# A Mamba layer with a mixture of experts on one core: gather and scatter moved in GpSimd's row, y's gating moved to the third stage, down weights in runs of 4 KB, x loaded a step ahead

## What is computed

```python
xn = layernorm(x)
# Mamba
u, gate = split(xn @ in_proj_w.T)
u = silu(conv4(u) + conv_b)                      # per channel, over the tokens
ts, B, C = split(u @ x_proj_w.T)
dt = softplus(ts @ dt_proj_w.T + dt_proj_b)
state[t] = state[t-1] * exp(dt * A) + dt * B * u # 16 states for each of 1024 channels
y = sum_over_states(state * C) + u * D
mamba = (y * silu(gate)) @ out_proj_w.T
# experts: for each (token, expert) pair among the top 6
moe = sum(score * (silu(xe @ w_gate) * (xe @ w_up)) @ w_down)
shared = (silu(xn @ sw_gate) * (xn @ sw_up)) @ sw_down
out = x + mamba + moe + shared
```

## Time and profile before

| | |
|---|---|
| median of 3 timed runs | 1342.65 us (1342.62 to 1343.42) |
| profiled execution | 1335.79 us, its span 1334.0 us |
| mean granted TensorE clock | 0.988 |
| busy: TensorE, VectorE, ScalarE, GpSimd | 1254.7, 1079.7, 899.2, 866.5 us |
| moved by DMA | 305.64 MB, mean 229 GB/s |

### The profile page before, as it was taken

How to read it: one execution, slowest core, us unless ns; L and a number is a source line. 1 busy time by engine, 2 the same in 40 slices (tenths; PEclk the granted TensorE clock), 3 DMA queues, 4 the chain that set the end, 5 groups by cost and what they waited for, 6 DMA issues and landing times.

```text
span 1334.0 us, 52998 instructions
## 1 busy us (share of the span) xinstructions
PE 1254.7 (94%) x21558; PEld 804.3 (60%) x21558; DVE 1079.7 (81%) x1235; ACT 899.2 (67%) x1925; POOL 866.5 (65%) x456
## 2 busy tenths in 40 slices
PE   6899999699999899999899999899999999999998
PEld 4777767455555455555455555455545678787876
DVE  5879889699899889998899999799999474646554
ACT  4666676487888878888788888678787242424343
POOL 3445458289889889898888988889989240303030
PEclk9999999799999999999999999999999999999999
DMA  8363554789999989999999999978898844032130
GB/s 271 124 258 129 213 213 141 242 264 281 308 265 318 287 228 318 293 274 306 267 286 301 268 307 289 311 253 270 260 315 264 281 161 154 36 106 84 64 125 31
DMA packets 131362, 305.64 MB, mean 229 GB/s; under 512 B 18272, under 2 KB 22368, under 8 KB 129504
## 3 DMA queue, kind: packets, MB, share of 16 engines
q1 hardware_dynamic: 123664, 285.92, 65.6%
q0 software_dynamic: 7632, 18.91, 7.1%
HBM read 213.78 MB, written 57.43 MB: 203 GB/s over the span
## 4 chain that ended last, share of the span: by engine, by line
PE 57%; DVE 9%; issue 7%; ACT 5%; DMA 2%; POOL 1%; ACTq 1%; DVEq 0%; SPq 0%; POOLq 0%
PE p_dBx L1367 16%; PE p_dBx L1425 7%; PE p_y L1376 7%; PE p_g L1353 6%; DVE state L1056 5%; PE p_g L1336 5%; PE p_u L1336 3%; PE p_y L1436 3%; PE p_g L1436 2%; PE p_u L1436 2%; PE p_dt L1436 2%; ACT dA L1206 2%; DVE out_operand_parts L1091 2%; DMA dt_blocks_even<-step_rows 1%; PE p_u L1322 1%
## 5 line engine op out<-in xcount | busy, mean ns | idle before, releaser
L1056 DVE TENSOR_TENSOR_SCAN state<-dA,state_carry,p_dBx 128x512 f32<-128x512 f32 x512 | 618.5, 1262 | 61.8 <-PE p_dBx L1367 61.5
L992 POOL TENSOR_TENSOR h_times_C<-state,C_bcast 128x1024 f32<-128x1024 f32 x128 | 304.3, 2379 | 63.1 <-DVE state L1056 62.1
L992 POOL TENSOR_TENSOR C_bcast<-state,C_bcast 128x1024 f32<-128x1024 f32 x128 | 315.9, 2624 | 23.1 <-DVE state L1056 22.4
L1367 PE MATMUL p_dBx<-B_diagonals,step_rows 64*32 64x128 f32 x16384 | 302.6, 275 | 24.4 <-DVE state L1056 12.9
L1367 PEld LDWEIGHTS p_dBx<-B_diagonals,step_rows 64*32 64x32 f32 x16384 | 235.3, 106 | 145.9 <-issue 142.7
L1206 ACT ACTIVATE dA<-dt_blocks_even,A_par 128x512 f32<-128x512 f32 x256 | 169.5, 709 | 27.5 <-DMA dt_blocks_even<-step_rows 27.5
L1206 ACT ACTIVATE dA<-dt_blocks_odd,A_par 128x512 f32<-128x512 f32 x256 | 169.5, 710 | 18.4 <-DMA dt_blocks_odd<-step_rows 16.2
L320 POOL TENSOR_TENSOR w_in_parts_lo<-C_bcast,w_in_parts_hi 128x512 fp32r<-128x512 f32 x64 | 94.4, 1477 | 99.2 <-ACT w_in_parts_hi L538 98.9
L1006 POOL TENSOR_TENSOR step_rows<-step_rows 128x512 f32<-128x512 f32 x16 | 22.5, 1435 | 182.4 <-DMA step_rows<-moe 182.4
L417 DVE SCALAR_TENSOR_TENSOR conv_out<-conv_in,conv_w,conv_out 128x512 f32<-128x512 f32 x96 | 107.2, 1124 | 20.7 <-ACT conv_out L562 18.4
L1353 PE MATMUL p_g<-w_down_pair,step_rows 128*64 128x512 f32 (+1 forms) x396 | 92.5, 602 | 0.0
(11 more groups left out here) (185 smaller groups left out, 2020.9 us busy)
## 6 DMA issues: line engine op xcount, KB each, us to landing
w_gate_pair<-in_w_gate SPq DMA_DIRECT2D x32, 1408.0 KB
w_up_pair<-in_w_up SPq DMA_DIRECT2D x32, 1408.0 KB
w_down_pair<-in_w_down SPq DMA_DIRECT2D x66, 512.0 KB
dt_blocks_odd<-step_rows SPq DMA_DIRECT2D x256, 64.0 KB
dt_blocks_even<-step_rows SPq DMA_DIRECT2D x240, 64.0 KB
w_down_pair<-in_w_down SPq DMA_DIRECT2D x33, 384.0 KB
g_d<-y_gated SPq DMA_DIRECT2D x33, 256.0 KB
sz_d<-silu_gate SPq DMA_DIRECT2D x32, 256.0 KB, 2.2
```

Of the source, the lines that this page charges most:

```text
L992: pool.tensor_tensor(hc[m][:, b, :, :], hb[:, q, :, :], Cb[:, NM * (c % 2) + GS * m:NM * (c % 2) + GS * m + GS, :], ALU.mult).then_inc(s_h ...
L1056: ins = dve.tensor_tensor_scan(hb[:, g % NBUF, s, :], dA[:, g % NBUF, s, :], pB[:, g % 2, :].rearrange("p (t s) -> p s t", s=GS)[:, s, :], ...
L1367: ins = pe.matmul(out[DB * p:DB * p + DB, half, j, :, :], dtxT[k, j * P + DB * b:j * P + DB * b + DB], diag[k, ND * cp + 2 * j + p // 2, a ...
```

## The change

- Gather: in each step it now stands before GpSimd's first product (and with it the wait for the tokens' copy `s_xT`); the scatter stands behind the sixth product, not the fifth.
- Gating: in stage 2 ScalarE only copies y out of its bank (`take_y`, in its seventh group), the bank starts from zero without x*D, and the stored y is ungated. In stage 3 VectorE does x*D + y and times the gate, for each of 32 tiles (`gating`), on inputs that SP loads (`gate_inputs`: x and gate tile, 256 KB each, two buffers). In the first chunk they stand 2, 2, 2, 1, 1 to the shared tiles; later chunks do three of them behind operand parts 11, 12 and 13 of the chunk before and five in the shared tiles. ScalarE's high part k waits for the gating of tile k.
- SP: the loads of the gates go from stage 2; x of step i+2 is loaded before the spread of dt. `gc` of the next chunk is loaded when part 7 is done, the stores of a chunk and the residual's loads stand between and behind the `gate_inputs` of the next.
- Down weights: laid out so that the two experts' rows are neighbours, one run of 4 KB a partition and third instead of two of 2 KB.
- VectorE's steps of the last chunk are written out instead of looped.

```diff
-GATHER_AT, SCATTER_AT = 0, 4
-DT_AT, GATE_AT, HH_AT = 1, 4, 5
+SCATTER_AT = 5
+DT_AT, HH_AT = 1, 5
+GATED_AHEAD = 3
+GATED_FIRST = [(0, 1), (2, 3), (4, 5), (6,), (7,), ()]
+GATED_IN_TILE = [(3,), (4,), (5,), (6,), (7,), ()]
...
-                    sp.dma_start(wd[0:k, :, m, :], io["w_down"][i][:, at:at + k, :].rearrange("a p h -> p a h")).then_inc(s_wd, 16)
+                    sp.dma_start(wd[0:k, m, :, :], io["w_down"][i][at:at + k, :, :]).then_inc(s_wd, 16)
...
+            def gate_inputs(c, d):
+
+                if ND * c + d >= 2:
+                    sp.wait_ge(s_g, ND * c + d - 1)
+                sp.dma_start(xa[:, d % 2, :], io["xt_d"][ND * c + d]).then_inc(s_gin[d % 2], 16)
+                sp.dma_start(sz[:, d % 2, :], io["sz_d"][ND * c + d]).then_inc(s_gin[d % 2], 16)
...
+                if i + 2 < STEPS:
+                    sp.wait_ge(s_dtx, i + 1)
+                    tile_in.load_xa(sp, i + 2)
...
                 if i + 1 < STEPS:
                     sp.wait_ge(s_dA, NG * i + 1)
                     spread_dt(i + 1)
-                sp.wait_ge(s_g, i + 1)
-                sp.dma_start(sz[:, :], io["sz_d"][i]).then_inc(s_sz, 16)
+                sp.wait_ge(s_y, i + 1)
                 sp.dma_start(io["g_d"][i], gb[:, 1 - i % 2, :]).then_inc(s_gst, 16)
...
             residual_inputs(0)
-            store_out(0)
             for c in range(1, NCH):
-                sp.wait_ge(s_kused, NK * c + 2)
+                sp.wait_ge(s_klo, 2 * NK * (c - 1) + 2 * ND)
                 sp.dma_start(gc, g_v[c]).then_inc(s_gc, 16)
+                for d in range(2 + GATED_AHEAD):
+                    gate_inputs(c, d)
+                store_out(c - 1)
+                for d in range(2 + GATED_AHEAD, ND):
+                    gate_inputs(c, d)
                 residual_inputs(c)
-                store_out(c)
+            store_out(NCH - 1)
...
             for i in range(STEPS):
                 c = i // ND
+                pool.wait_ge(s_xT, i + 1)
+                gather(i + 1)
                 pool.wait_ge(s_C, 32 * ND * (c + 1))
...
-                dve.wait_ge(s_sum, 2 * n + 2)
-                dve.tensor_tensor(gb[:, u, :], pY[:, :], sz, ALU.mult).then_inc(s_g, 1)
...
+            def gating(c, d):
+
+                if d == 0:
+                    dve.wait_ge(s_gc, 16 * c + 16)
+                dve.wait_ge(s_gin[d % 2], 16 * ND * c + 32 * (d // 2 + 1))
+                dve.scalar_tensor_tensor(gc[:, d, :], xa[:, d % 2, :], Dp[:, d:d + 1], gc[:, d, :], ALU.mult, ALU.add).then_inc(s_yD, 1)
+                dve.wait_ge(s_yD, ND * c + (d + 1))
+                dve.tensor_tensor(gc[:, d, :], gc[:, d, :], sz[:, d % 2, :], ALU.mult).then_inc(s_g, 1)
...
                     w_lo(NI * c + (m + 2), (m + 2) % NI)
+                    for d in GATED_FIRST[m] if first else GATED_IN_TILE[m]:
+                        gating(c, d)
                     if m in (NI - 3, NI - 2):
                         k_lo(c, m - (NI - 3))
...
-                act.wait_ge(s_g, i + 1)
-                act.activation(pY[:, :], xa[:, u, :], ACT.Copy, scale=d).then_inc(s_xD, 1)
+            def take_y(n, u):
+
+                act.wait_ge(s_gst, 16 * n + 16)
+                act.wait_ge(s_sum, 2 * n + 2)
+                act.activation(gb[:, u, :], pY[:, :], ACT.Copy).then_inc(s_y, 1)
...
-                    pe.wait_ge(s_xD, i + 1)
+                    pe.wait_ge(s_y, i + 1)
                     sum_states(i, 0, 0)
```

133 lines of the change are left out of this document (67 added, 66 removed).

## The result

The changed kernel took 1323.55 us (median of 4 runs, 1321.1 to 1329.42) against 1342.63 for the kernel before on the same chip: a ratio of 0.986 (95% interval 0.982 to 0.990), 19 us faster. The same pair, timed again on two occasions, gave 0.990 (0.987 to 0.994) and 0.990 (0.987 to 0.993), 13 and 14.5 us faster.

What follows compares the result with a forecast made beforehand. The scan stage was taken as nearly level between TensorE (ahead), VectorE, GpSimd and DMA, the third stage as TensorE's alone. Scan stage -12 and third stage +16 gave +4 on 1342.65: 1347 us, range 1330 to 1357.

Steps and rivals of the forecast that it cites:

- GpSimd's order: Scan stage: moving gather and scatter leaves the last product's end unchanged, 0 us, between -1 and +2.
- x a step ahead: Scan stage: half of VectorE's 5.2 us of waits for x goes, -2.5 us, between 0 and -5.2.
- fewer bytes: Scan stage: dropping the gates' load, with 4 KB runs included, gives -2 us, between 0 and -10.2.
- gating out of the scan stage: Scan stage: TensorE's waits on x*D go, -5 us, and four waits for scans in the last chunk shrink, -2.4.
- third stage, first chunk: Third stage: late inputs of pairs 2 and 3 delay tile 4, +11.0, with backlog and lower clock +14.1 us together.
- the backlog behind the gap: Third stage, first chunk: VectorE's queued pairs, products and operand parts delay TensorE's parts 2 by +1.4 us more.
- later chunks: Third stage: GpSimd's residual sums fall into the operand parts, about 0.7 us more a chunk, +2 in all, bounds -3 and +6.
- A: Rival: TensorE's scan stage gaps come from full DMA queues, so that stage gives -26: 1333 us, chance 0.14.
- B: Rival: third stage inputs of pair 2 come in time because queues share engines more evenly: 1334 us, chance 0.12.
- D: Rival: dt comes late in the scan stage, at ScalarE's dA before group 0, +10 instead of 0: 1357 us, chance 0.07.
- E: Rival: GpSimd's sums hold VectorE up where the third stage's pairs run, +5: 1352 us, chance 0.06.

Runs made afterwards that it cites:

- chip 9: The chip of the first four experiments (GpSimd order variants of both kernels), where the kernel before took 1328.7 us, against 1341.8 to 1345.6 on all others.
- k_order_x_first: Kernel before with gather ahead of the first product, scatter behind the sixth, and x loaded right behind the spread of dt: 0.993 of before.
- k_inputs_first: Changed kernel with inputs of pairs 2 and 3 issued ahead of the shared down weights, all gating inputs ahead of the x loads: 0.983 of before.
- k_x_late: Changed kernel with the load of x back where it was, GpSimd's new order kept: 0.996 of before, 1335.7 us.
- k_scatter: Kernel before with the scatter alone moved behind the sixth product: 1.024 of before.
- k_order: Kernel before with GpSimd's new order alone, gather ahead of the first product and scatter behind the sixth: 1.027 of before.

## Why the prediction was wrong, step by step

**Failed: "GpSimd's order ... 0, between -1 and +2".** This is the largest error. I followed when the products end and who waits for their sums, and took no account of what the indirect DMAs do to others. On one chip the old order costs 20 us with x late (1.014 against 0.996), and with x ahead the scatter's old place alone 0.9%, 12 us, the gather's 0.1%. The scatter acts in two ways: GpSimd's issue of it stretches TensorE's short matmuls, and with the new place x is late unless it is loaded sooner. The prediction's own had a trace of it, 10.2 us of "issue" before dBx in 18 places, put down to full queues at -2; after the change it is 7.5 us in 4. Most of the cost stood in no idle column.

**Failed: "x a step ahead ... -2.5, between 0 and -5.2".** The rows showed a wait of 5.2 us and I took it as all there was to win. With the new order the load was worth 6.5 to 8 us (0.996 to 0.990), because that order makes x late: 23.5 us of waits. Its slack, not its wait, was what counted: x was issued at 21 us of a 23.8 us step, and a step that becomes shorter, or another transfer in that place, turns the slack into a wait.

**Failed in kind: the sum of separate terms.** The parts act on each other. The new order pays in the stretched places and costs in a late x, so its worth depends on where x is loaded, and on the chip: on the kernel before it cost 2.7% on chip 9, and gained 0.7% on another with x moved ahead of the up weights; in the pair above it gained 1.7%. On the chip of that pair the kernels form a chain: before 1341.8 us; gating out, fewer bytes and longer runs 1356.2, of which the third stage is +20; the new order 1335.7; x a step ahead 1329.1. A part forecast by its present wait is sized too small when other parts go with it.

**Right in size: gating out of the scan stage**, -5 - 2.4 and -2 for fewer bytes, -9.4. Alone (old order, x late) the scan stage was 775.3 us against 779.8 and 782.6: -5 to -7. The stretched places are 11 us longer in that trace than in the first one of before, so the gating's own share was larger and the agreement is partly chance. With the other limits gone it seems worth more: against `k_order_x_first`, whose 31 steps take 751.4 us, the changed kernel's take 720.8 and 727.6, and in ordinary steps 2.87 - 2.21 = 0.66 us of it is dBx 5, 6 and the wait for x*D; x is loaded sooner too. The 4 KB runs gave nothing that shows. The Trainium skill, "DMA: Bandwidth & Descriptors", section "Why small descriptors are slow (HBM only)", leaves 2% between these lengths, on a fifth of the bytes. That is, as an estimate from its figure, 0.4% of the stage's DMA time, 3 us or 0.2%; the runs are known to 0.3% and can neither show nor refute it.

**Right: third stage, first chunk, +14.1.** Measured +14.3, the gap 10.29 against 11.0, the start of pair 2 within 0.2 us, and the queue's order is the cause, shown by `k_inputs_first`. That the sum fits so closely is luck: the backlog behind the gap, put at 1.4, was 0.1 (1.9 us of waits in the operand parts against 1.8 before); tile 4 took 8.41 us instead of 5.63 at a mean granted clock of 0.66, 2.8 for 1.7; and tile 0 took 0.9 longer (8.21 against 7.32), which was not foreseen. Nor was the wait before tile 0, 5.72 against 2.37 us: VectorE's first low weights take 4.01 us beside GpSimd's last products. It is counted in the scan stage, whose other gain is so 36 us.

**Right in mechanism, mis-sized: later chunks, +2 (bounds -3 and +6).** Measured +6.7. GpSimd's sums do fall into the operand parts and VectorE takes 1.77 us there instead of 0.69; TensorE then stood at four parts in each of the three chunks (the first 1.32 to 1.37, then three of about 0.4), 2.6 us a chunk, where I had put 0.7 more than before. The first of the four:

```profile
1134.41 0.93 PE L1466 MATMUL p_y<-out_operand_parts 128*128 128x512 f32 x3 [1.37 <-DVE out_operand_parts L1105]
```

**The rivals.** A had the sign and was nearest (1333), but its mechanism, full queues, is not it: the stage moved 284 GB/s after and 282 before, and with fewer bytes and the old order the step stayed at 23.8 us. B did not happen: pair 2's inputs came late. D and E did not decide.

**What stays open.** Why chip 9 hardly shows the stretch; whether the change gains anything there, since the changed kernel was not run on it. That TensorE's instructions are supplied late is only argued: the traces show late starts without a cause. Both places old with x ahead were timed on chip 9 alone. The first step of a chunk (28.6 to 29.4 us after) was not studied.

## What to carry to other kernels

Compare the duration of the same group of instructions from step to step, not its idle time alone: a matmul group that takes 3.0 us here and 1.9 there waits for something the idle columns do not show. For every load note the slack between its landing and its use; when a change shortens the loop or moves a transfer, the load with the least slack is the next wait. When several resources are within a few per cent of each other, forecast the parts together, try them one by one, and keep each pair on one chip: the four runs on chip 9 nearly hid the main cause, because what it removes hardly exists there. A trace of the baseline on the same chip would have shown it at once.

## What the runs showed of the hardware

- In the traces of all chips but one, TensorE's short matmuls were stretched while GpSimd issued an indirect DMA (1.00 us for a gather, 1.60 for a scatter). It goes by the start of the issue: 64 short matmuls of 1.09 us took 1.09 with the gather starting 0.9 us or more ahead of them, 1.19 with 0.8, 1.46 with 0.5, 1.58 with 0.4 (medians of dBx 2 in 15 traces), and 1.73 with a scatter 0.4 ahead (dBx 7). A sum of 16 took 2.9 us instead of 1.85 with the gather 0.22 to 0.26 us ahead, and 1.85 with it 0.1 us ahead or just behind its start. Beside long matmuls (the down product, 2.73 us) nothing was seen.
- On chip 9, in four traces, gathers and scatters at these distances left the sum at 1.85 us and dBx 7 at 1.08 to 1.31. Only a gather that started with dBx 2 or within it stretched that, to at most 1.53; on the others it was 2.0 to 2.4 there.
- The scatter's packets left 2.2 us behind its issue when it stood behind the fifth product. Behind the sixth it was 5.3 to 5.6 us in the changed kernel, `k_x_late` and the two versions that move the gather alone, 4.8 in `k_scatter` and 3.1 to 3.4 in the two with x first (medians). In the step of the changed kernel shown above SP issued the up and down weights from 370.0 to 372.5 us, right behind the scatter at 369.59.
- In a step of `k_order` (from 343.3 us), where dBx 3 and 4 with a wait took 6.3 us instead of 2.0 (TensorE stood 3.28 us of it), the transposes behind them took 1.04 instead of 0.59 and the up product 3.9 instead of 2.5, 1.9 us more on top of 4.3; the mean granted clock from 347.0 to 358.5 us was 0.72.
